# Linear attention and recurrence re-tiled from 112 to 128 tokens, with the causal mask moved to GpSimd

## The reference

```
t  = tokens(x)
q, k, v = split(LN(t) @ W.T + b)
q = elu(q) + 1 ; k = elu(k) + 1
num_t = sum over s <= t of (q_t . k_s) v_s
den_t = sum over s <= t of (q_t . k_s) + 1e-6
t = t + num / den
```

## Time and profile before

| | us |
|---|---|
| median of three runs | 2030.25 (2029.51 to 2030.74) |
| the profiled execution | 2031.14 |
| its span, first to last instruction | 2029.5 |
| PE busy | 1923.1 (95%) |
| DVE busy | 1677.6 (83%) |
| ACT busy | 1465.6 (72%) |
| POOL busy | 1290.2 (64%) |

### The profile page before, as it was taken

How to read it: one execution, slowest core, us unless ns; L and a number is a source line. 1 busy time by engine, 2 the same in 40 slices (tenths; PEclk the granted TensorE clock), 3 DMA queues, 4 the chain that set the end, 5 groups by cost and what they waited for, 6 DMA issues and landing times. The chain is left out here.

```text
span 2029.5 us, 64530 instructions
## 1 busy us (share of the span) xinstructions
PE 1923.1 (95%) x20434; PEld 1672.5 (82%) x20434; DVE 1677.6 (83%) x5427; ACT 1465.6 (72%) x3774; POOL 1290.2 (64%) x1760
## 2 busy tenths in 40 slices
PE   4999999999999997999999999999999995699997
PEld 2888888888888886899999999999999993466664
DVE  7888888888888885799999999999999992355554
ACT  3777777777777775799999999999999981122221
POOL 3888888888888885444544444444444445577772
PEclk9999999999999999899999999999999996899998
DMA  4343434443434322122222222222222212366663
GB/s 137 106 110 106 109 108 110 106 112 104 113 103 111 94 78 73 38 62 62 59 61 61 59 62 60 59 63 59 59 63 59 59 51 63 109 199 199 187 210 110
DMA packets 228620, 190.53 MB, mean 94 GB/s; under 512 B 19264, under 2 KB 187552, under 8 KB 228448
## 3 DMA queue, kind: packets, MB, share of 16 engines
q1 hardware_dynamic: 228448, 188.22, 33.3%
HBM read 111.08 MB, written 77.07 MB: 93 GB/s over the span
## 5 line engine op out<-in xcount | busy, mean ns | idle before, releaser
L830 POOL TENSOR_SCALAR la_spread<-la_mv 112x4 f32<-112x4 f32 x231 | 54.6, 236 | 388.5 <-DVE la_mv L916 388.1
L536 POOL TENSOR_TENSOR wa_prob<-wa_prob,wa_peak 128x784 f32<-128x784 f32 x128 | 194.5, 1520 | 118.4 <-DVE wa_peak L425 118.4
L788 ACT ACTIVATE la_raised<-k_psum,la_bqk 128x224 f32<-128x224 f32 x448 | 200.6, 448 | 73.9 <-PE k_psum L682 73.9
L838 POOL TENSOR_TENSOR la_ln<-la_spread,k_exponent 112x4 f32<-112x4 f32 x231 | 239.5, 1037 | 1.8 <-ACT la_u L771 0.3
L1274 ACT ACTIVATE main_y<-k_psum,sc_cols 128x448 f32<-128x448 f32 x112 | 70.9, 633 | 209.1 <-PE k_psum L1215 209.1
L682 PE MATMUL k_psum<-la_uT,la_wt 128*128 128x224 f32 x896 | 211.2, 358 | 0.0
L771 ACT ACTIVATE la_u<-la_xc,la_ln 112x128 f32<-112x128 f32 x448 | 201.1, 515 | 13.3 <-POOL la_ln L842 13.2
L805 ACT ACTIVATE la_u<-la_tn,la_ln 112x128 f32<-112x128 f32 x448 | 201.0, 515 | 10.2 <-POOL la_ln L842 10.2
L543 POOL TENSOR_TENSOR wa_prob<-wa_prob,wa_inv 128x784 f32<-128x784 f32 x128 | 194.8, 1522 | 10.1 <-DVE wa_inv L389 10.1
L789 ACT ACTIVATE la_positive<-k_psum,la_bqk 128x224 f32<-128x224 f32 x448 | 200.8, 448 | 0.0
L417 DVE TENSOR_TENSOR wa_prob<-k_psum,wa_bias 128x784 f32<-128x784 f32 x128 | 124.9, 976 | 83.1 <-PE k_psum L272 83.1
(11 more groups left out here) (147 smaller groups left out, 5879.2 us busy)
## 6 DMA issues: line engine op xcount, KB each, us to landing
wa_xw<-in_x_tok SPq DMA_DIRECT2D x128, 224.0 KB, 2.7
wa_xT<-in_x_cm SPq DMA_DIRECT2D x128, 196.0 KB, 2.5
la_xc<-x SPq DMA_DIRECT2D x224, 112.0 KB, 2.0
t<-la_tn SPq DMA_DIRECT2D x224, 112.0 KB, 2.0
main_tb<-t SPq DMA_DIRECT2D x28, 896.0 KB, 6.0
out<-main_ob SPq DMA_DIRECT2D x28, 896.0 KB, 7.6
x<-wa_y SPq DMA_DIRECT2D x128, 112.0 KB
x<-wa_y SPq DMA_DIRECT2D x128, 56.0 KB
```

The lines of the kernel that those rows point to most:

```text
L536: nc.gpsimd.tensor_tensor(s, s, peak[:, k % S, :].unsqueeze(2).broadcast_to([128, PAIRS * HEADS, WIN]), ALU.subtract).then_inc(lowered, 1)
L788: nc.scalar.activation(raised[:, k, j, :], src, ACT.Exp, bias=bqk[:, j:j + 1])
L838: nc.gpsimd.tensor_tensor(rstd, spread[:, :], exponent[0:CH, 0:4], ALU.pow).then_inc(rooted, 1)
```

## The change

**Linear attention** works in units of two chunks of 128 tokens: 196 units instead of 224. 3136 is not a multiple of 128, so an image can begin in the middle of a chunk; such a chunk has a second mask, and its `outer` and `numerators` use half of the rows. All loops are written out in full, with no hardware loop.

- The layer norm's mean is taken off and its scale applied on POOL (`normalise`, `normalise2`) in place of ACT. `statistics` keeps only the addition and the power.
- The bias of queries, keys and values is folded into the weights before the loop: `uT` is u + 1, and the weights get (bias - column sum)/128 added. With it comes the 1 of elu + 1, so that `combine` is min(max(z, 1), exp(z - 1)), read from PSUM; ACT makes one exp of 512 columns and no relu.
- The scores are copied out of PSUM by ACT (`inner_copy`), and POOL multiplies the copy by the mask in SBUF (`mask_inner`).
- The state is added up in PSUM by `outer`, one chunk after the other, and ACT copies it out after each (`keep_state`). DVE loses `advance`, `carry`, `inner_out` and `values_out`; the last is ACT's.

**Recurrence**: 32 segments of 98 steps, 512 columns, [128, 4, SB, 128] with SB = 7 (main) and 6 (warm). The shift is folded into the weights, so POOL does one multiplication per block. The scale table is turned by PE, copied by ACT, written to DRAM and read back in the scan's layout.

The core of the diff (`chunks` and `keep`, the sizes of the tiles and the unchanged waits are left out):

```diff
+        P = 128
+        UNITS = B * T // (2 * P)
+        steps = range(-4, UNITS + 9)
 PE:
                 def queries_and_keys(n):
-                    at_least(pe, qk_raised, n)
+                    at_least(pe, qk_out, n)
                 def scores(n):
-                    at_least(pe, a_out, n)
+                    at_least(pe, a_copied, n)
+                def outer(n, a):
+                    c = 2 * n + a
+                    if not inside(n, UNITS) or ends(c):
+                        return
+                    at_least(pe, kept, outers(c))
+                    part = slice(64, P) if splits(c) else slice(0, P)
+                    fresh = begins(c) or splits(c)
+                    nc.tensor.matmul(b_kv[:, 0:E], kt[part, n % S, a, :], ve[part, n % S, a, :], start=fresh, stop=True,
+                                     skip_group_check=True).then_inc(kv_ready, 1)
+                for n in steps:
+                    queries_and_keys(n)
+                    turn_keys(n - 1)
+                    turn_tokens(n + 1)
+                    outer(n - 2, 0)
+                    numerators(n - 3)
+                    moments(n - 8)
+                    outer(n - 2, 1)
+                    values(n + 1)
+                    scores(n)
 ACT:
+                def inner_copy(n):
+                        act.wait_ge(a_ready, n + 1)
+                        at_least(act, num_ready, n - S + 1)
+                        nc.scalar.activation(aT[:, n % S].rearrange("p a b -> p (a b)"), b_at[:, 0:2 * P], ACT.Copy).then_inc(a_copied, 1)
+                for n in steps:
+                    inner_copy(n - 1)
+                    exps(n)
+                    keys_out(n - 1)
+                    turned_out(n + 1)
+                    keep_state(n - 2, 0)
+                    values_out(n + 1)
+                    keep_state(n - 2, 1)
 POOL:
+                def statistics(n):
+                    pool.wait_ge(aggregated, n + 1)
+                    nc.gpsimd.tensor_scalar(spread[:, :], mv[:, n % S].rearrange("p l a m -> p (l a) m")[:, :, 1], LN_EPS, None,
+                                            ALU.add).then_inc(spread_out, 1)
+                    pool.wait_ge(spread_out, n + 1)
+                    nc.gpsimd.tensor_tensor(rstd[:, n % S, :], spread[:, :], exponent[:, 0:4], ALU.pow).then_inc(rooted, 1)
+                def normalise(n):
+                    pool.wait_ge(rooted, n + 1)
+                    at_least(pool, u_turned, n - S + 1)
+                    for a in range(2):
+                        last = nc.gpsimd.tensor_scalar(u[:, n % S, a, :], xc[:, n % XS, a, :], mv[:, n % S, 0, a, 0:1],
+                                                       rstd[:, n % S, a:a + 1], ALU.subtract, ALU.mult)
+                    last.then_inc(normed, 1)
+                def mask_inner(n):
+                        pool.wait_ge(a_copied, n + 1)
+                            last = nc.gpsimd.tensor_tensor(aT[:, n % S], aT[:, n % S], masks[:, 0, :].unsqueeze(1).broadcast_to([P, 2, P]), ALU.mult)
+                        last.then_inc(a_out, 1)
+                for n in steps:
+                    statistics(n + 3)
+                    mask_inner(n - 1)
+                    normalise(n + 2)
+                    normalise2(n - 5)
 DVE:
+                link(nc.vector.tensor_scalar(bias[:, 0:2 * C], bias[:, 0:2 * C], 1.0, None, ALU.add))
+                dve.wait_ge(summed, 1)
+                link(nc.vector.tensor_tensor(fold[:, :], bias[:, :], b_u[:, 0:3 * C], ALU.subtract))
+                nc.vector.scalar_tensor_tensor(wt[:, :], fold[:, :], 1.0 / C, raw[:, :], ALU.mult, ALU.add).then_inc(folded, 1)
+                for n in steps:
+                    measure(n + 3)
+                    denominators(n - 3)
+                    combine(n)
+                    invert(n - 3)
+                    aggregate(n + 3)
+                    attend(n - 3)
 recurrence:
+                sp.wait_ge(table_out, 1)
+                sp.dma_start(flat.rearrange("(g c p) -> c g p", g=4, p=128), turned[:, :, :]).then_inc(flat_out, 16)
+                sp.wait_ge(flat_out, 16)
+                sp.dma_start(rstd[:, :, :], flat.rearrange("(g p s) -> p g s", g=NG, s=STEPS)).then_inc(rstd_in, 16)
+                sp.wait_ge(rstd_in, 16)
-        scan(nc, t2, None, CH - WARM, fT, vT, shift_bn, rstd, shift, start, final, ident, bank, "warm")
+        scan(nc, t2, None, STEPS - WARM, 6, fT, vT, shift_bn, rstd, start, final, ident, bank, "warm")
-        scan(nc, t2, out, 0, fT, vT, shift_bn, rstd, shift, start, final, ident, bank, "main")
+        scan(nc, t2, out, 0, 7, fT, vT, shift_bn, rstd, start, final, ident, bank, "main")
```

More of the change, by code:

```diff
@@ L635, in _ @@
             def _(sp):
[L636 to L643, removed]
+                sp.dma_start(raw[:, :], attn_wt).then_inc(consts, 16)
@@ L650, in store @@
+                def store(n):
+                    if not inside(n, UNITS):
                         return
                     sp.wait_ge(attended, n + 1)
[L652 to L657, removed]
+                    sp.dma_start(rows(t2, n), tn[:, n % XS]).then_inc(stored[n % XS], 16)
@@ L668, in turn_tokens @@
-                def turn_tokens(n, k):
-                    if not inside(n, NC2):
+                nc.tensor.matmul(b_u[:, 0:3 * C], ones[:, :], raw[:, :], start=True, stop=True).then_inc(summed, 1)
+                def turn_tokens(n):
+                    if not inside(n, UNITS):
                         return
@@ L747, in moments @@
                     mm.then_inc(counted, 1)
[L749 to L758 removed]
+                pe.wait_ge(folded, 1)
@@ new lines, in aggregate @@
+                def aggregate(n):
+                    if not inside(n, ROWS):
+                        return
+                    dve.wait_ge(measured, n + 1)
+                    at_least(dve, normed, min(UNITS, n - S + 1))
+                    at_least(dve, normed2, n - S - AHEAD + 1)
+                    for which, m in ((0, n), (1, n - AHEAD)):
+                        if inside(m, UNITS):
+                            for a in range(2):
+                                last = nc.vector.bn_aggr(mv[:, n % S, which, a, :], stats[:, n % S, which, a, :])
+                    last.then_inc(aggregated, 1)
@@ L1156, in _ @@
             def _(sp):
-                def step(j, k):
+                for j in range(-3, NB + 2):
                     if inside(j + 3, NB):
-                        kl = 1 - k
                         if out is not None:
@@ L1276, in _ @@
-                pipeline(act, step, **run)
+                for t in range(NT):
+                    act.wait_ge(v_done, t + 1)
+                    if out is not None:
+                        at_least(act, y_turned, t - 1)
+                    nc.scalar.activation(y[:, t % 2, :], b_state[t % 2][:, 0:COLS], ACT.Sigmoid, bias=shift_bn).then_inc(y_made, 1)
         if repeated:
```

585 lines of the change are left out of this document (251 added, 334 removed).

## The result

The changed kernel takes 2506.34 us (median of 4 runs, 2505.64 to 2507.35) against 2030.11 us (median of 4): the ratio is 1.2346, 95% interval 1.2325 to 1.2368. The change costs 476.2 us, where 278 were forecast. The profiled execution took 2505.64 us for a span of 2503.9 us. The direction and the mechanism were as forecast; the size was not, and the time lies above the range.

The account below looks back on a forecast made before the run. A closed ring of waits in linear attention was to bind at 5.72 us a step, 1121 us instead of 850.5; with +3 for edges and +4 for the recurrence, 2029.5 became 2307 us of span, forecast 2308 us, range 2225 to 2420.

Parts of the forecast that it names:

- The ring: Linear attention: TensorE, VectorE and GpSimd wait for one another in a circle within one step; 5.72 us a step.
- handovers: Linear attention's waits between engines: TensorE to VectorE 0.20 us, VectorE to GpSimd 0.08, GpSimd to TensorE 0.05.
- The step that failed: GpSimd's price for normalising 128 columns in linear attention, worked out from L529: 0.377 us, bounds 0.22 and 0.677.
- if a GpSimd operation costs twice what its row says: Sign, in the profile after, that the forecast is wrong; expected were a mask of 0.74 and normalisations of 0.38 us.
- The clock: Rival in linear attention: TensorE's idling halves its clock, its work of 7.98 us a step binds, 2751 us; chance 0.04.
- The edges of the stage: Linear attention's bias folding before the loop, with fill and drain otherwise alike: +3 us, give or take 10.
- The recurrence: Stage after linear attention: scan steps, loads, first blocks, last store and scale table together cost +4 us.
- The three terms: Recurrence: doubled transfers add 4 us each for the main first load, the warm first load and the last store.
- The block of 3584 columns: Recurrence, main scan: GpSimd's first block is one pass of 6.3 us instead of two of 3.6 with a wait.
- The ring is not closed: Rival in linear attention: numerators over combine to scores binds at 4.11 us, 1992 us, or TensorE alone, 1969; chance 0.09.
- lighter TensorE work: Linear attention: TensorE's own work is 3.99 us a unit, 782 us for 196 units, 68 less than before.

Follow-up runs that it names:

- e1: Changed kernel with normalise(n+2) moved to the head of GpSimd's step, ahead of statistics(n+3) and the mask; 2201.73 us.
- e4: Changed kernel plus a block of isolated GpSimd operations, six calls of each kind, between linear attention and recurrence; 2536.08 us, run once.
- e2: Changed kernel with both GpSimd normalisations as multiply and add instead of subtract and multiply, output not the reference's; 2323.43 us.
- e5: Changed kernel with four extra matmuls of 256 columns on TensorE ahead of turn_tokens in each step; 2467.44 us.
- e6: Changed kernel with normalise at the head of GpSimd's step and normalisations as multiply and add, output not the reference's; 1981.09 us.
- e7: Changed kernel with normalise first on GpSimd, mask on VectorE from PSUM, normalisation as scale plus shift, computing the reference; 1982.91 us.
- e8: As e7, with combine ahead of denominators on VectorE; 1957.39 us.
- e3: Changed kernel with the mask on VectorE straight from PSUM, without ScalarE's copy and GpSimd's product; 2328.83 us.

## Why the prediction was wrong in size and right in mechanism

**The ring** is as the prediction drew it: the same six parts in the same order, and their sum is the step. TensorE 1.39 (1.40 forecast), handovers 0.20, 0.09 and 0.05 (0.20, 0.08, 0.05), VectorE 1.23 (1.26), and on GpSimd the power 1.04 and the mask 0.73 (0.74). e1 shows it by undoing: with one line moved the wait for the aggregate no longer delays anybody.

**The step that failed** is the price of a normalisation, "L529 does the same on 392 columns in 0.677 us; with 0.24 for four columns, 0.377 for 128". L529 does not do the same. It is a multiply and an add, the new instruction a subtract and a multiply, and the argument took the duration by the name of the instruction, its shape and its column operands, but not by its operations. That both ends of its bounds (0.22 and 0.677) came from the same row made the range too narrow as well: 0.797 lies above them. Even with the right row the number was low; multiply and add takes 0.443 for 128 columns (e4). By its two widths its fixed part is 0.34 us, where the prediction took the 0.24 of a call on four columns. The prediction itself named "if a GpSimd operation costs twice what its row says" as a sign of being wrong, but gave it no chance. In the ring this term is 1.58 instead of 0.71, +0.87 of the 1.10 us by which the mean step exceeds the forecast (6.82 against 5.72); the ring's other parts take 0.02 off. e2 confirms it from inside the kernel. Two small slips of its working matter little: 0.24 for four columns and 0.677 for 392 give 0.380 for 128, not 0.377, and 845 us over 223 waits are 3.789 us a step, not 3.797, which makes 1.7 us over the stage.

**The clock** is nearly all of the rest, 6.82 - 6.57 = +0.25 us (e5: 0.23; the images' starts are in what is left). The prediction had it only as a rival of all or nothing, half clock throughout, 2751 us; its argument against, one stretch at 1.00 with a single wait of 1.40 us, nearly held for waits of that size and not for the 2.2 us that came. Here the two errors are one: with the normalisation near its forecast, e2 has waits of 1.54 us and one fall of the clock behind the stage's start. The Trainium skill, page "TensorE: Matmul & The Clock Gate", section "HAM oscillation", describes gaps that return in a loop and put the clock down each time; the trace shows it in about every sixth step (32 of some 190), not in each.

**The sum.** 196 x 1.10 = +215.6 us. The edges of the stage, forecast at +3, came to -5.7: 1359.5 - 196 x 6.82 = 22.8 us against 879.0 - 850.5 = 28.5. That makes linear attention 207 us longer than forecast.

**The recurrence** was to cost 4 us and gains 6.1. The rows of the main scan's first load and first block, and of the wait for the last store:

```profile
2217.05 3.90 SPq L1175 DMA_DIRECT2D main_tb<-t  x4
```

```profile
2224.29 6.18 POOL L1189 TENSOR_TENSOR main_ub<-main_tb,sc_scan_rstd 128x3584 f32<-128x3584 f32 x1 [33.80 <-DMA main_tb<-t]
```

```profile
2495.51 0.68 DVE L1103 TENSOR_TENSOR sc_gap<-sc_final,sc_start 128x496 f32<-128x496 f32 x1 [6.15 <-PEq L1167]
```

The load landed after 2224.29 - 2217.05 = 7.24 us, 1.1 more than the half-sized one of the earlier trace rows, where 4 more were forecast; the warm load 6.3 after its issue, where the smaller one took 5.8; the last store is waited for 6.15 us against 4.96, +1.2 instead of +4. The transfers as a whole grew by more than these three: the pages of the profile give, before and then after,

```profile
main_tb<-t SPq DMA_DIRECT2D x28, 896.0 KB, 6.0
out<-main_ob SPq DMA_DIRECT2D x28, 896.0 KB, 7.6
```

```profile
main_tb<-t SPq DMA_DIRECT2D x14, 1792.0 KB, 8.0
out<-main_ob SPq DMA_DIRECT2D x14, 1792.0 KB, 11.9
```

(number, size, median us from issue to landing). A load of twice the size takes 2.0 us longer, half of what the prediction took. A store takes 4.3 longer, near what it took; why only 1.2 of this shows at the end stays open.

The three terms, two first loads and the last store, were together over-sized by 9.2 of the 10 us. The block of 3584 columns is 6.18 us, forecast 6.3. Linear attention and recurrence together are 207 - 10 = 197 of the 198 us that the time lies above the forecast.

**The rivals.** "The ring is not closed" is out for the kernel as changed, but its numbers held once the ring was opened: 4.11 us a step in e6 and e7, and 4.00, TensorE alone, in e8. The change's lighter TensorE work was real all along and is what e8 collects.

**What stays open**: why the clock falls in just those steps in which it does, and a few other steps between 6.6 and 7.0 us. Of the 66 steps after 1676 us, 12 take 6.65 with TensorE's part 0.08 longer, and in two of 6.9 VectorE idles 0.4 us ahead of `combine`.

## What to carry to other kernels

Before an instruction is put behind a wait in an in-order queue, follow what it releases around all engines: if the circle comes back to that wait within one step, the step is the circle's length, whatever the engines' busy shares say, and moving one independent piece of work ahead of the wait may be worth more than any faster instruction (here 305 us for one line). Price an instruction by a row with the same operations, not only the same shape and operand kinds; where there is none, let the bounds reach well past the nearest row. And ask of each forecast wait of TensorE what rows of the same length show of the clock: here some 190 waits of 1.5 us brought it down once (e2) or three times (e3), as many of 2.2 us 32 times.

## What the runs showed of the hardware

- GpSimd's `tensor_scalar` costs by its pair of operations: for 128 and 392 columns with column operands, measured alone (e4), subtract and multiply 788 and 1667 ns; multiply and add 443 and 662; add and multiply 441 (128); subtract alone 597 (128); subtract and multiply with constants 640 (128). The Trainium skill, page "GPSIMD Engine Reference", section 4.1, has operations with one input at roughly line rate. By these rows that can't hold for both pairs: multiply and add takes 0.83 ns a column, subtract and multiply 3.3.
- The granted clock fell to 0.50 for some 3 us in 32 of some 190 steps where TensorE waited about 2.2 us of 6.57. It fell once where TensorE waited 1.54 of 5.88 (e2: 157.3 us in 102 times), three times where it waited 1.55 of 5.88 (e3), and not at all where it waited 0.54 of 6.59 (e5).
- Of the recurrence's transfers, loads of 1792 KB landed 8.0 us after their issue (median) and stores 11.9; those of 896 KB took 6.0 and 7.6.
